# A gated feed-forward layer with adapters: two stages with h in DRAM, and gate and up as seven block products

## The reference

```python
def _lora_linear(x, W, A, B, adapter_indices):
    base = jnp.einsum('bsd,df->bsf', x, W)
    Ai, Bi = A[adapter_indices], B[adapter_indices]
    return base + jnp.einsum('bsr,brf->bsf', jnp.einsum('bsd,bdr->bsr', x, Ai), Bi)
gate = _lora_linear(x, Wg, Ag, Bg, idx)
up = _lora_linear(x, Wu, Au, Bu, idx)
h = jax.nn.silu(gate) * up
x = x + _lora_linear(h, Wd, Ad, Bd, idx)
x = x + jnp.einsum('bct,bcd->bdt', x, weights[idx])   # 64 x 64 per sequence, over its 64 tokens
```

## Time and profile before

| | us |
|---|---|
| median of 3 runs | 1343.55 (1340.61 to 1347.19) |
| span of the profiled execution | 1334.9 |
| PE busy in it | 1304.7 (98%) |
| DVE, ACT, POOL busy | 651.8, 520.5, 198.5 |
| DMA | 166.56 MB, mean 125 GB/s |

### The profile page before, as it was taken

How to read it: one execution, slowest core, us unless ns; L and a number is a source line. 1 busy time by engine, 2 the same in 40 slices (tenths; PEclk the granted TensorE clock), 3 DMA queues, 4 the chain that set the end, 5 groups by cost and what they waited for, 6 DMA issues and landing times.

```text
span 1334.9 us, 21342 instructions
## 1 busy us (share of the span) xinstructions
PE 1304.7 (98%) x6464; PEld 1098.6 (82%) x6464; DVE 651.8 (49%) x1032; ACT 520.5 (39%) x954; POOL 198.5 (15%) x438
## 2 busy tenths in 40 slices
PE   4999999999999999999999999999999999999996
PEld 3888888888888888888888888888888888888884
DVE  3644455444654446444465344644446444554442
ACT  3533344333433334434344334343334333433330
POOL 5310031100311012110221102101032000320000
PEclk9999999999999999999999999999999999999998
DMA  7745283552835436372453725527264262732210
GB/s 243 211 104 156 71 158 131 128 132 92 168 122 128 130 93 151 114 166 94 113 143 124 166 87 118 170 76 180 79 140 146 86 142 81 163 139 71 94 48 31
DMA packets 38605, 166.56 MB, mean 125 GB/s; under 512 B 10418, under 2 KB 11442, under 8 KB 32562
## 3 DMA queue, kind: packets, MB, share of 16 engines
q1 hardware_dynamic: 27136, 134.24, 38.2%
q0 software_dynamic: 11008, 30.42, 7.8%
q10 hardware_dynamic: 434, 1.58, 0.3%
HBM read 157.82 MB, written 8.39 MB: 125 GB/s over the span
## 4 chain that ended last, share of the span: by engine, by line
PE 97%; DMA 1%; ACT 1%; DVE 0%; issue 0%; POOL 0%; DVEq 0%; POOLq 0%
PE gate_ps L613 9%; PE out_ps L613 9%; PE gate_ps L614 9%; PE out_ps L614 9%; PE gate_ps L615 9%; PE out_ps L615 9%; PE up_ps L615 9%; PE up_ps L614 9%; PE up_ps L613 9%; PE td_ps L673 5%; PE up_ps L632 5%; PE gate_ps L632 5%; PE misc_ps L698 2%; PE misc_ps L711 2%; PE out_ps L688 1%; DMA xt_raw<-xt 1%
## 5 line engine op out<-in xcount | busy, mean ns | idle before, releaser
L475 DVE TENSOR_TENSOR w_lo<-raw,w_hi 128x512 fp32r<-128x512 f32 x384 | 265.2, 692 | 352.0 <-ACT ad_hl L370 231.1
L370 ACT ACTIVATE w_hi<-raw 128x512 fp32r<-128x512 f32 x384 | 239.7, 626 | 289.2 <-PE out_ps L615 246.1
L370 ACT ACTIVATE h_hi<-h_f 128x512 fp32r<-128x512 f32 x128 | 80.9, 632 | 372.4 <-DVE h_f L590 372.4
L613 PE MATMUL gate_ps<-xt_hi,w_hi 128*128 128x512 f32 x512 | 205.1, 401 | 17.0 <-DVE w_lo L475 15.3
L613 PE MATMUL up_ps<-xt_hi,w_hi 128*128 128x512 f32 x512 | 202.0, 395 | 0.0
L614 PE MATMUL gate_ps<-xt_lo,w_hi 128*128 128x512 f32 x512 | 201.5, 394 | 0.0
L613 PE MATMUL out_ps<-w_hi,h_hi 128*128 128x512 f32 x512 | 201.4, 393 | 0.0
L614 PE MATMUL out_ps<-w_lo,h_hi 128*128 128x512 f32 x512 | 201.3, 393 | 0.0
L615 PE MATMUL gate_ps<-xt_hi,w_lo 128*128 128x512 f32 x512 | 200.2, 391 | 0.0
L615 PE MATMUL out_ps<-w_hi,h_lo 128*128 128x512 f32 x512 | 199.7, 390 | 0.0
L614 PE MATMUL up_ps<-xt_lo,w_hi 128*128 128x512 f32 x512 | 199.3, 389 | 0.0
(11 more groups left out here) (70 smaller groups left out, 1637.4 us busy)
## 6 DMA issues: line engine op xcount, KB each, us to landing
raw<-packed SPq DMA_DIRECT2D x128, 768.0 KB, 4.4
bq_raw<-b_gu SPq DMA_DIRECT2D x240, 128.0 KB, 5.9
xt_raw<-xt POOLq DMA_DIRECT2D x8, 1024.0 KB, 9.7
x<-x POOLq DMA_DIRECT2D x8, 1024.0 KB, 6.5
y_out_dram<-y POOLq DMA_DIRECT2D x32, 256.0 KB, 2.8
bd_raw<-b_d POOLq DMA_DIRECT2D x128, 32.0 KB, 6.4
bq_raw<-b_gu SPq DMA_DIRECT2D x16, 96.0 KB, 3.4
ad_all<-a_d ACTq DMA_DIRECT2D x1, 1024.0 KB, 11.6
```

The costliest lines, as they stand in the source:

```text
L370: return act.activation(dst, src, ACT.Copy)
L475: return dve.tensor_tensor(dst, src, hi.bitcast(F32), ALU.subtract)
L613: pe.matmul(ps, st[0], mv[0], start=start, stop=False)
```

## The change

The program is written anew, in two stages, without loops (all steps are unrolled).

**Stage 1** computes h for all tokens: 4 groups of 1024 tokens by 16 chunks, 64 steps. Gate and up of 2 x 512 tokens are one block product of two by two: the operands' halves are first summed (of x once a group: `x_add` on DVE, seven operands `xo_hi`, `xo_lo`; of the weights in each step: `w_add`, four sums of 128 x 256), and then seven products of 256 x 128 by 512 tokens replace eight. In the order of PE (`step`): P1, P5, the adapters' part of one result into a bank of its own (`l22`), P6, P2, P7, P3, P4, each product with 6 matmuls, each of the four results with 4 matmuls of 256 columns for the adapters. ACT copies P1, P5 and U2 out of PSUM (`keep_p1`, `keep_p5`, `keep_u2`), DVE adds (`make_c11`, `make_u3`, `make_c22`, `make_c12`), and ACT and DVE make h from them. SP stores h to DRAM (`store_h`, 512 KB a step in rows of 1 KB).

The adapters' B is split once, in the first 8 steps: per piece of two chunks POOL loads it, ACT and DVE split it (`b_hi`, `b_lo`), SP stores both parts side by side in DRAM (`store_b`). `gather_b` takes from there, per piece and group, 16 slots by two DMAs of 64 KB into one of two `bq` slots. `lora_a` is plain f32 now.

**Stage 2** computes the rest in 16 pairs of 128-token tiles. The split down weights stay in SBUF for all pairs (`wd_hl`, 16 chunks of 1152 columns), in the room that x and the weights had in stage 1; the pair's adapter columns are written between their blocks, so that the matmuls of 320 and 288 columns give the adapters' product along with a half of the down product. h comes back from DRAM in 64 batches of four chunks and is split then (`h_hi`, `h_lo`). `turn` transposes the small product by a matmul with the identity; `lora_down` and `mix_tile` follow during the next pair.

The diff, cut to what sets these orders:

```diff
-GROUPS = BATCH * SEQ // TOK
-STEPS = GROUPS * CHUNKS
+GROUPS, GT, HALF = 4, 1024, 512
+STEPS = GROUPS * CH
+SLOTS = GT // SEQ
+PIECE = 2
...
+            def load_w(s):
+                if s >= 2:
+                    sp.wait_ge(w_lo_done, 3 * (s - 2) + 1)
+                sp.dma_start(raw[s % 2][:, :], packed[s % CH]).then_inc(w_in[s % 2], 16)
...
+            def store_h(s):
+                g, c = divmod(s, CH)
+                sp.wait_ge(h1_done, s + 1)
+                sp.wait_ge(h2_done, s + 1)
+                sp.dma_start(h_dram[4 * g:4 * g + 4, :, c, :].rearrange("q p t -> p q t"),
+                             h_f[s % 2][:, :].rearrange("p (q t) -> p q t", q=4)).then_inc(h_stored[s % 2], 16)
...
+            def gather_b(n):
+                g, k = divmod(n, PIECES)
+                sp.wait_ge(b_stored, 16 * (k + 1 if g == 0 else PIECES))
+                if n >= 2:
+                    sp.wait_ge(p4_done, 2 * n - 2)
+                for b in range(SLOTS):
+                    a = number(sp, g * SLOTS + b)
+                    for half in range(2):
+                        r = half * QR + (b % QS) * RANK
+                        sp.dma_start(bq[n % 2][r:r + RANK, b // QS, :, :].bitcast(F32).rearrange("r k c -> r (k c)"),
+                                     b_dram[k, bass.ds(a, 1)].rearrange("a r c -> (a r) c"))\
+                            .then_inc(bq_in[n % 4], 16)
...
+            store_b(0)
+            gather_b(0)
+            for s in range(STEPS):
+                if s + 2 < STEPS:
+                    load_w(s + 2)
+                if s >= 1:
+                    store_h(s - 1)
+                if 0 < s < PIECES:
+                    store_b(s)
+                if s == 1:
+                    gather_b(1)
+                if s and s % 2 == 0 and s + 2 < STEPS:
+                    gather_b(s // 2 + 1)
...
+                if more:
+                    w_hi_raw(s + 1)
+                if s:
+                    keep_p1(s)
...
+                keep_u2(s)
...
+                if 0 < s < PIECES:
+                    b_hi(s)
...
+                    pe.matmul(tile[:, 0:HD + 2 * TR], h_hi, w[:, wide[0]:wide[0] + HD + 2 * TR],
+                              start=first, stop=False, skip_group_check=True)
```

More of the change, by code:

```diff
@@ L111, in cond_resid_kernel @@
[L111 to L122, removed]
@@ L267, in _ @@
+            load_h(0)
+            store_h(STEPS - 1)
+            load_h(1)
+            load_h(2)
+            for c in range(11, CH):
+                load_wd(c)
+            load_h(3)
+            for n in range(PAIRS * BATS):
+                p, q = divmod(n, BATS)
+                if q == 0:
+                    load_bd(p)
+                if q == 1 and p + 1 < PAIRS:
+                    load_ad(p + 1)
+                if n + 4 < PAIRS * BATS:
+                    load_h(n + 4)
         @block.gpsimd
@@ L346, in _ @@
[L346 to L360 removed]
+            for q in range(QUADS):
+                gather_a(0, q)
@@ L746, in last, with prod @@
-            def last():
-                down(GROUPS * CHUNKS - 1, 1, False, True)
-                lora_down(GROUPS - 1)
-                for j in range(TILES):
-                    mix_tile(GROUPS - 1, j, LAST_BANKS[j])
-            run_groups(pe, chunk, first, last)
+            def prod(bank, s, w, k, start):
+                a = w * WB
+                for kk in range(2):
+                    wc, xc = slice(a + kk * P, a + (kk + 1) * P), slice(kk * HALF, (kk + 1) * HALF)
+                    st = w_hi[s % 2][:, wc], w_lo[s % 2][:, wc]
+                    mv = xo_hi[k][:, xc], xo_lo[k][:, xc]
+                    pe.matmul(bank, st[0], mv[0], start=start and kk == 0, stop=False, skip_group_check=True)
+                    pe.matmul(bank, st[0], mv[1], start=False, stop=False, skip_group_check=True)
+                    m = pe.matmul(bank, st[1], mv[0], start=False, stop=kk == 1, skip_group_check=True)
+                return m
@@ new lines, in lora @@
+            def lora(bank, s, u, pair, start):
+                g, c = divmod(s, CH)
+                b = bq[(s // PIECE) % 2]
+                for part in range(2):
+                    for i in range(2):
+                        q = pair * 2 + i
+                        a = part * WB + u * P
+                        m = pe.matmul(bank[:, i * QT:(i + 1) * QT], b[:, q, c % PIECE, a:a + P],
+                                      t_st[u][g % 2][:, q * QT:(q + 1) * QT], start=start and part == i == 0,
+                                      stop=part == i == 1, skip_group_check=True)
+                return m
@@ L755 @@
+            for j in range(2):
+                turn(PAIRS - 1, j)
+            for j in range(2):
+                lora_down(PAIRS - 1, j)
+            for j in range(2):
+                mix_tile(PAIRS - 1, j)
 def kernel(x, itok_B_0_7, L0_cond_Wg, L0_cond_Wu, L0_cond_Wd, L0_cond_Ag, L0_cond_Bg, L0_cond_Au,
```

1361 lines of the change are left out of this document (805 added, 556 removed).

## The result

The changed kernel takes 1541.74 us (median of 4 runs, 1537.79 to 1546.49), the kernel before 1343.77 on the same chip: 1.149 times as long, with a 95% interval of 1.145 to 1.153. The profiled execution has a span of 1536.1 us and a mean granted clock of 0.915 (0.995 before).

A forecast was written before the change was run, and what follows sets the result against it. SP's issuing of gathers was to bound stage 1: ramp to gather 5 at 218 us, 26 rounds of 27.7 to 938, stage 1's end at 1006, stage 2 and tail to 1464, plus 8.65: 1473 us, range 1410 to 1530.

The forecast's parts named there:

- The bound moves from PE to SP's queue: Stage 1: one round of SP's issuing takes 27.7 us against 22.9 for PE's two steps, so SP sets the pace.
- Rival (a): SP's queue in stage 1: issue doesn't bound, PE does; a slot under 1.33 us; 1247 us, faster; chance 0.05.
- The size of a gather: SP's queue in stage 1: 16 slots at 1.62 us each hold SP for 26.0 us a piece.
- rival (d): All queues: a long straight program makes them wait for instructions, 1 us a step, 60 more; "(d) or else" 0.05.
- What stands between two gathers: SP's queue in stage 1: two weight loads and two stores of h at 0.42 each, 1.7 us a round.
- the lead: SP's queue: 0.76 us from the end of a weight load to a slot's first DMA, counted within the slots.
- PE's return and the clock: Stage 1: PE's way back allows 53 us per two rounds against 55.4; PE waits 4.8 of 27.7 us.
- the slack: Stage 1: 2.4 us that should absorb the clock's drop in PE's waits, which cost about 2 us.
- Rival (c): Stage 1: each gather waits for a step behind the gather before, rounds stay 35.8, 1683 us; 0.10 with steps toward it.
- The landing: Gathers in stage 1: the last DMA lands about 3.5 us after the issue ends.
- The ramp: First group of stage 1: pieces are split, stored, read back in rounds of 35.8 us; gather 5 starts at 218.
- Stage 2: After stage 1: PE bounds it, 389 us for the tile-chunks plus smaller terms, waits and tail; 458 in all.

The follow-up runs named there:

- e1: Changed kernel with a group's 16 adapter numbers read once into SP registers, not again for each piece: 1355.84 us, 1.011 of the kernel before.
- e11: Changed kernel with each slot reading its adapter number twice, no DMA added: 1817.38 us, 1.354 of the kernel before.
- e2: Changed kernel with slots 8 to 15 of each gather issued by POOL and 0 to 7 by SP: 1349.7 us, 1.006 of the kernel before.
- e3: Changed kernel with the stores of h issued by POOL instead of SP: 1501.76 us, 1.120 of the kernel before.
- e7: Changed kernel with only the order of the first pieces' splits, stores and gathers and POOL's loads changed: 1506.01 us, 1.123 of the kernel before.
- e10: Changed kernel with numbers read once a group, reordered first pieces, second weight load inside the gather, 4 KB rows of h, later x split: 1297.49 us, 0.967.
- e4: Changed kernel with weight loads and h stores placed singly between slots in 20 gathers: 1502.17 us, 1.121 of the kernel before.
- e9: Changed kernel storing h as 128 rows of 4 KB instead of 512 of 1 KB: 1536.61 us, 1.146 of the kernel before.
- e12: Changed kernel with each weight load issued as two DMAs of 256 KB: 1545.76 us, 1.153 of the kernel before.

## Why the forecast was right, and where it failed

**The bound moves from PE to SP's queue: right, and shown.** e1 and e11 change nothing but SP's reads and move the total by -186 and +276 us; e2 moves half of a gather to another queue, for -192. Rival (a), that issue doesn't bound, falls with e11 above all. The Trainium skill, page "DMA: Bandwidth & Descriptors", section "Issuing engines are not separate DMA queues", calls sequencer time usually small relative to the DMA itself. For one DMA this trace agrees: its issue took 0.32 to 0.36 us in most slots, 0.8 with its share of the read, and it landed 2.1 us after (median). The prediction set the issue of 16 against the landing of one, which isn't a fair comparison. What decides is that landings overlap and issues in one queue don't: 32 of them took 25.4 us.

**The size of a gather: right.** 25.24 from the first to the last DMA by the slot of the earlier trace rows, 25.44 measured as a mean over gathers 5 to 31, with about 0.3 of it in the pauses described under rival (d). The slot of a 16-row transfer of another tensor was a good proxy.

**What stands between two gathers: the step that failed.** The forecast said "1.7 more" for two weight loads and two stores of h, "nearest that, 0.42", and the lead of 0.76 stood in the slots: 2.46. It measured 5.13, of which 0.43 are loads of x and for stage 2 that the sum carried elsewhere. The missing 2.2 us a round over 26 rounds are 58 of the 69 us by which the total was off, and 63 with the 0.2 that a gather took longer. In the round shown, 4.47 us pass from 246.87 to 251.34: of the excess of 2.0, the fourth issue is 1.0 (1.43, not 0.42), the lead to the first slot 0.7 (1.44, not 0.76, with a read of 0.89), and gaps and the third issue are 0.3. Over all 26 rounds the 2.2 are 1.2 for the issues and the gaps between them, 0.6 for the lead and 0.5 for waits for h, which the forecast put at nothing. So the mechanism held, and a term of the sum was mis-sized: a round of 27.7 us for a measured 30.57, above even its upper bound of 29.4. The fault in method is plainer than the cause: stores of h were not in the trace, yet the upper bound of the round let only the slots vary (1.54 to 1.73) and gave the unseen part its nearest row as its only value. A row that stands alone in the trace (at 15.45) says nothing of four in a row. The range was narrow besides: by the bounds that the forecast lists upwards (53, 15 and 10) it would have reached 1551, and it stopped at 1530.

**PE's return and the clock: held, barely.** The forecast gave PE 4.8 us of waiting a round, ended by the piece and by P1's copy; measured are (829 - 696) / 27 = 4.9. PE in the changed kernel, at one piece (start, modelled us, what, and in brackets the idle time ahead and what ended it):

```profile
492.54 0.74 PE L862 MATMUL ps<-t_st,bq 128*128 128x256 f32 x4 [1.70 <-DMA bq<-b_dram]
...
496.65 0.80 PE L850 MATMUL ps<-xo_hi,w_hi 128*128 128x512 f32 x1 [3.37 <-ACT p_s L394]
...
501.08 0.63 PE L851 MATMUL ps<-xo_lo,w_hi 128*128 128x512 f32 x1
501.51 0.63 PE L852 MATMUL ps<-xo_hi,w_lo 128*128 128x512 f32 x1
...
502.48 0.40 PE L850 MATMUL ps<-xo_hi,w_hi 128*128 128x512 f32 x1
502.71 0.39 PE L851 MATMUL ps<-xo_lo,w_hi 128*128 128x512 f32 x1
```

The two waits are there, 1.70 for the piece and 3.37 for P1's copy. Behind the second, matmuls of 512 columns follow each other every 0.43 us (501.08, 501.51) and from 502.48 on every 0.23: the lower clock level for twelve of them, 5.3 us in place of 2.7, so 2.6 lost. I had expected about 2 us for it, in the slack. SP never waited for the fourth product, so the slack did take it, in a round that was 2.9 us longer than forecast; e3, with a round 1.4 us shorter, shows five such waits. Rival (c) was close by, but didn't decide.

**The landing: too long.** I took 3.5 us from 96 KB transfers; the 64 KB ones landed in 2.1. Behind the ramp it isn't on SP's path. In the ramp it is part of every round, and too long by 1.4 us there.

**The ramp: right in kind; the size is partly luck.** Gather 5 at 220.9 against 218; the single steps differ by up to 10 us (108.5 for 118.5, 152.7 for 154, 190.1 for 190). Gather 2 came 10 us early, and the round behind it, which also has the four loads of x, took 44.2 us and not 35.5, so that the two errors cancel. Gather 31 starts at 1015.7 against 949.5, so 3 of these 66 us are the ramp and 63 the rounds. e7 shows what the order costs: 36 us.

**Stage 2: right.** It takes 467 us from the last product of stage 1 to the end, against 458. To the 66 us by which gather 31 is late these add 9. Between gather 31 and that product 3 us fewer pass than forecast, and the median lies 5.6 us and not 8.65 above the span: 69 in all. Six matmuls of a tile-chunk, from one of 320 columns to the next:

```profile
1100.37 0.31 PE L961 MATMUL ps<-wd_hl,hh 128*128 128x320 f32 x1
...
1101.12 0.32 PE L961 MATMUL ps<-wd_hl,hh 128*128 128x320 f32 x1
```

0.75 us, where the line between 256 and 512 columns gave 0.761: 6 us less in all. The Trainium skill, page "TensorE: Matmul & The Clock Gate", section "Back-to-back issue gap", gives the rule that the prediction set beside it as the gap of an isolated matmul. That it comes out lower here (0.695) says little against it. The waits for x1 are 8.4 (10 forecast). What was missing is one wait of 5.9 us of ACT for the second batch of h right after the transition, while the DMA engines were 0.96 busy at 324 GB/s, and a lower clock until 1100.

**Rival (d)**, queues that wait for instructions in a long straight program: there is something like it, but small. At every 128th of its recorded instructions SP stands for 0.34 to 0.35 us (once 0.42) without a wait that the profile shows; the line at 484.55 above is one. Between gathers 5 and 31 that happens 27 times, 9.3 us or 0.36 a round, which the forecast's sum had at nothing. The kernel before, which loops, has none of that length between 221 and 1050 us. That they are waits for instructions isn't shown. On PE nothing needs (d): e10 has it busy for 753 of 770 us (60 to 830) in the same unrolled code. No run took it apart alone.

## To carry to other kernels

When a change tiles work more finely, count what each issuing queue has to do per round, reads of numbers included, and hold it against the step of the engine that bounds now. A price of 1.6 us for a slot of two DMAs was small change at 272 DMAs and most of the result at 1024. Read a value once if it repeats, keep large transfers apart in a queue, and put the one that a blocked engine needs ahead of the long run and not behind it. And where the trace doesn't show an operation, give it an upper bound well above its nearest row, above all if it will stand in a place (third or fourth in a row) in which no row stands.

## What the runs showed that I had not expected

- In 14 of 26 rounds the fourth DMA of 512 KB in a row held SP for 1.2 to 1.5 us where the first three took 0.4 to 0.5, and the register read behind it took up to 1.24 in place of 0.27. With small DMAs between them (e4), or behind a wait of 2.2 us or more, all took about 0.4. With eight in a row the longest took 0.95. Rows of 4 KB in place of 1 KB (e9) and 256 KB in place of 512 (e12) made little difference.
- At every 128th instruction SP paused for 0.34 us, in the unrolled kernels (the changed one, e1, e10, e11).
- A read of one number into a register and the instructions on it cost SP 0.54 us (e11), more than a DMA's issue of 0.32 to 0.36.
- After waits of 1.7 and 3.4 us with 0.7 of work between them, PE ran 5.3 us at the lower clock level, which cost 2.6 us on top of the waits.
